# Layer 1's attention: the values product by batch in tiles of 64 rows, in two halves around the value projection

## What is computed

```python
qh = (q_in @ wq + bq).reshape(b, q_len, H, K)
kh = (kv_in @ wk + bk).reshape(b, t, H, K)
vh = (kv_in @ wv + bv).reshape(b, t, H, K)
kh = jnp.concatenate([kh, jnp.broadcast_to(bias_k, (b, 1, H, K))], axis=1)
vh = jnp.concatenate([vh, jnp.broadcast_to(bias_v, (b, 1, H, K))], axis=1)
scale = jnp.sqrt(jnp.asarray(K, q_in.dtype))
logits = jnp.einsum('bqhk,bthk->bhqt', qh, kh) / scale
weights = jax.nn.softmax(logits, axis=-1)
ctx = jnp.einsum('bhqt,bthk->bqhk', weights, vh).reshape(b, q_len, H * K)
return ctx @ wo + bo
```

## Time and profile before

| | |
|---|---|
| median of 3 runs | 1749.71 us (1749.53 to 1749.79) |
| the profiled execution's own time | 1759.38 us |
| its span in the trace | 1757.7 us |
| TensorE busy | 1592.3 us, 91% |
| VectorE busy | 920.9 us, 52% |
| ScalarE busy | 739.9 us, 42% |
| GpSimd busy | 429.2 us, 24% |
| mean granted clock of TensorE | 0.959 of full |

### The profile page before, as it was taken

One profiled execution on the slowest core, in us unless ns is written; L12 is line 12 of the kernel. 1 busy time (PEld: TensorE's weight loads), 2 busy tenths in 40 slices (PEclk: granted clock), 3 DMA queues, 4 the chain that ended last, 5 costly groups with the idle time before them and its releaser, 6 DMA issues. The chain is left out here.

```text
span 1757.7 us, 33325 instructions
## 1 busy us (share of the span) xinstructions
PE 1592.3 (91%) x13484; PEld 1355.6 (77%) x13484; DVE 920.9 (52%) x1912; ACT 739.9 (42%) x1393; POOL 429.2 (24%) x518
## 2 busy tenths in 40 slices
PE   5978999999999969999999999839978877999797
PEld 3656888888888858888888888729857756888597
DVE  6874444343434454252525353574469975776443
ACT  4653434343434334444343434332246643544321
POOL 2012020010110030110200200160058867663400
PEclk9998999999999989999999999959979988999899
DMA  3021010010000030000000100010050000000001
GB/s 101 1 64 45 1 49 1 7 43 1 25 13 1 1 101 9 25 25 1 25 25 1 37 1 1 31 39 1 0 133 1 2 1 2 3 3 2 1 1 48
DMA packets 48464, 38.24 MB, mean 22 GB/s; under 512 B 10626, under 2 KB 45384, under 8 KB 48200
## 3 DMA queue, kind: packets, MB, share of 16 engines
q1 hardware_dynamic: 48328, 36.30, 7.0%
HBM read 34.20 MB, written 2.10 MB: 21 GB/s over the span
## 5 line engine op out<-in xcount | busy, mean ns | idle before, releaser
L939 DVE TENSOR_REDUCE att_rmax<-psum 128x6 f32<-128x390 f32 (+1 forms) x96 | 49.2, 512 | 401.2 <-PE psum L771 401.2
L914 ACT ACTIVATE att_q_sb<-psum,split_cols 128x512 f32<-128x512 f32 x128 | 88.1, 688 | 295.8 <-PE psum L807 295.0
L852 PE MATMUL psum<-att_wo_hi,att_ot_hi 128*128 128x256 f32 x512 | 149.4, 292 | 2.8 <-DVE att_ot_lo L968 2.8
L852 PE MATMUL psum<-att_wo_lo,att_ot_hi 128*128 128x256 f32 x512 | 144.8, 283 | 0.0
L852 PE MATMUL psum<-att_wo_hi,att_ot_lo 128*128 128x256 f32 x512 | 144.8, 283 | 0.0
L835 PE MATMUL psum<-att_pt,att_v_sb 128*128 128x128 f32 x1024 | 122.2, 278 | 1.0 <-ACT att_pt L923 1.0
L835 PEld LDWEIGHTS psum<-att_pt,att_v_sb 128*128 128x128 f32 x1024 | 116.8, 192 | 3.3 <-issue 1.5
L917 ACT ACTIVATE att_k_sb<-psum,split_cols 128x512 f32<-128x512 f32 x128 | 88.2, 689 | 71.3 <-PE psum L807 71.3
L807 PE MATMUL psum<-split_feat_hi,att_wqk_hi 128*128 128x512 f32 x256 | 105.5, 412 | 12.8 <-DVE att_pt L933 12.8
L721 POOL CAST att_wqk_hi<-w_stage_qk 128x512 fp32r<-128x512 f32 x28 | 17.2, 613 | 401.4 <-PE psum L807 397.0
L977 DVE TENSOR_TENSOR g_x_res<-psum,g_x_res 128x256 f32<-128x256 f32 x128 | 54.3, 424 | 110.6 <-PE psum L852 77.7
(11 more groups left out here) (295 smaller groups left out, 4130.6 us busy)
## 6 DMA issues: line engine op xcount, KB each, us to landing
ln_wo<-in_L_xattn_wo SPq DMA_DIRECT2D x2, 2048.0 KB
w_stage_qk<-in_L_xattn_wq SPq DMA_DIRECT2D x32, 128.0 KB, 2.3
w_stage_qk<-in_L_xattn_wk SPq DMA_DIRECT2D x32, 128.0 KB, 2.8
w_stage_vo<-in_L_xattn_wv SPq DMA_DIRECT2D x8, 512.0 KB, 3.9
w_stage_vo<-in_L_xattn_wo SPq DMA_DIRECT2D x8, 512.0 KB, 3.9
...
```

The costliest lines, as they stand in the source:

```text
L852: mm = pe.matmul(o_ps[p % 2], a, b, start=(h == 0 and t == 0), stop=(not last and h == HG - 1 and t == 2))
L914: act.activation(q_sb[:, h, :], q_ps[:, :], ACT.Identity, bias=G.cols[:, i - 1, head:head + 1]).then_inc(q_ready, 1)
L939: dve.tensor_reduce(rmax[:, a:b], s_ps[group][:, :, :], X_AXIS, ALU.max).then_inc(max_done, 1)
```

## The change

- `pt` loses its zero halves: it is now 64 keys of either batch above one another and 64 columns for each chunk and head. The clearing of `pt` and its semaphore go. ScalarE copies each transposed pair with one instruction of 128 rows in place of two of 64.
- `context` takes a half (`pp`): two chunks. For each chunk, head and batch (`u`) it multiplies 64 rows of `v_sb` (128 stationary columns) with 64 columns of `pt`: 16 matmuls a half, 32 a block. Batch 0 of a chunk uses rows 0 to 63 and writes the first bank of `c_ps`, batch 1 rows 64 to 127 and the second bank.
- `c_ps` is now two banks, which are also those of the transposes (`t_ps`) and, for odd chunks, of the outputs. So half 1 has to wait until half 0 is copied out (`ot_ready`, now counted in halves).
- `context(j - 2, 0)`, `values(j - 1, 0)`, `context(j - 2, 1)`, `values(j - 1, 1)` follow one another, where there was `context(j - 2)` and `values(j - 1)`.
- `context_high` and `context_low` copy a half at a time (1024 elements a row), and `ot_hi` and `ot_lo` are laid out by chunk. The first output chunk waits for half 0, the others for half 1.
- The softmax steps on ScalarE and VectorE are put in another order around these copies.

```diff
-        pt = m.sb("pt", [P, HG, 2, 2, 2, T])
-        ot_hi, ot_lo = (m.sb(n, [P, HG, BLK], F32R) for n in ("ot_hi", "ot_lo"))
+        pt = m.sb("pt", [P, HG, 2, 2, T])
+        ot_hi, ot_lo = (m.sb(n, [P, PPB, HG, P], F32R) for n in ("ot_hi", "ot_lo"))
...
-        t_ps = [m.ps(f"t_ps{n}", (P, 2, 2, P)) for n in range(2)]
+        c_ps = m.ps("c_ps", (P, 2, PPB // 2, HG, T))
+        t_ps = c_ps.rearrange("p u c h t -> p u (c h t)").rearrange("p n (h a t) -> p n h a t", h=2, a=2)
...
-        c_ps = [q_ps, k_ps, flat[0], flat[1]]
-        o_ps = [o_full[:, 0:D], flat[1][:, 0:D]]
+        o_ps = [o_full[:, 0:D], c_ps[:, 1, 0, :, :].rearrange("p h t -> p (h t)")]
...
+        def by_half(ot, pp):
+            return ot[:, 2 * pp:2 * pp + 2, :, :].rearrange("p c h (u t) -> p u (c h) t", u=2)
...
-                def context(j):
-                    for copied in v_ready:
-                        pe.wait_ge(copied, 2 * j + 2)
-                    pe.wait_ge(q_ready, HG * min(j + 2, NI))
-                    pe.wait_ge(k_ready, HG * min(j + 2, NI))
-                    for h in range(HG):
-                        pe.wait_ge(pt_ready, 4 * j + 2 * (h // 2) + 2 if h < 2 else 4 * j + 4)
-                        for p in range(PPB):
-                            mm = pe.matmul(c_ps[h][:, p * P:(p + 1) * P], v_sb[:, p, h * K1:(h + 1) * K1],
-                                           pt[:, h, p // 2, p % 2, :, :].rearrange("p u t -> p (u t)"), start=True, stop=True)
-                        mm.then_inc(c_psum, 1)
+                def context(j, pp):
+                    pe.wait_ge(pt_ready, 2 * j + 2)
+                    if pp:
+                        pe.wait_ge(ot_ready, 2 * j + 1)
+                    else:
+                        for copied in v_ready:
+                            pe.wait_ge(copied, 2 * j + 2)
+                        if j:
+                            pe.wait_ge(x_added, PPB * j)
+                    for p in (2 * pp, 2 * pp + 1):
+                        for h in range(HG):
+                            for u in range(2):
+                                rows = slice(T * u, T * u + T)
+                                mm = pe.matmul(c_ps[:, u, p % 2, h, :], v_sb[rows, p, h * K1:(h + 1) * K1],
+                                               pt[rows, h, pp, p % 2, :], start=True, stop=True)
+                    mm.then_inc(c_psum, 1)
...
-                pe.wait_ge(pt_zero, 1)
...
-                        context(j - 2)
+                        context(j - 2, 0)
                     if 1 <= j <= NI:
-                        values(j - 1)
+                        values(j - 1, 0)
+                    if j >= 2:
+                        context(j - 2, 1)
+                    if 1 <= j <= NI:
+                        values(j - 1, 1)
...
-                            for u in range(2):
-                                half = slice(T * u, T * u + T)
-                                act.activation(pt[half, 2 * pair:2 * pair + 2, :, :, u, :].rearrange("p h a r t -> p (h a r) t"),
-                                               t_ps[pair][half, :, :, :].rearrange("p h a (r t) -> p (h a r) t", r=2),
-                                               ACT.Copy).then_inc(pt_ready, 1)
+                            act.activation(pt[:, 2 * pair:2 * pair + 2, :, :, :].rearrange("p h a r t -> p (h a r t)"),
+                                           t_ps[:, pair, :, :, :].rearrange("p h a t -> p (h a t)"), ACT.Copy).then_inc(pt_ready, 1)
...
-                dve.memset(pt[:, :, :, :, :, :].rearrange("p h a r u t -> p (h a r u t)"), 0.0).then_inc(pt_zero, 1)
...
+                def context_low(j, pp):
+                    dve.wait_ge(ot_high, 2 * j + pp + 1)
+                    dve.tensor_tensor(by_half(ot_lo, pp), c_ps[:, :, :, :, :].rearrange("p u c h t -> p u (c h) t"),
+                                      by_half(ot_hi, pp).bitcast(F32), ALU.subtract).then_inc(ot_ready, 1)
```

83 lines of the change are left out of this document (40 added, 43 removed).

## The result

| kernel | median of its runs, us | lowest to highest | beside the kernel before |
|---|---|---|---|
| before, runs beside the changed kernel | 1749.62 | 1748.61 to 1749.79 (4) | |
| changed | 1768.53 | 1767.43 to 1770.94 (4) | ratio 1.0112, interval 1.0099 to 1.0124 |

A forecast was written before the change was run, and what follows sets the result against it. TensorE's own time was taken to bound each pass. Terms 14.1 + 1.1 + 3.4 - 5.5 + 0 = +13.1 us, carried over to the runs' median of 1749.71, gave 1762.8 us; range 1752 to 1780, the sum's own 1757 to 1768.

The forecast's parts named there:

- The product gains nothing: Values product in each pass: a pair of half-depth records takes 0.112 us, as one full record does; 0 us.
- pairs at 0.060: Rival on the values product: half-depth loads take half the time or overlap further, 53 us less, 1710 us; chance 8%.
- loads in turn: Rival on the values product: loads of two row halves take turns, 0.224 a pair, 115 us more, 1878 us; 3%.
- Changes of tile shape: Borders between full and row tiles around the product: 0.47 us a pass, 30 passes, 14.1 us more.
- the turned bias: Last group, 3 passes an attention: bias transposes between scores and product add a full-to-row change, 6 x 0.19 = 1.1 us.
- The new wait: Second half's product in a pass waits until the first half is copied out; 0.5 us spare, so 0 us.
- The rival in which VectorE's copy comes too late: Before a pass's second half: VectorE's strided copy takes 2.32, 18 us more in all, 1781 us; chance 11%.
- The start: Start of each attention: TensorE no longer waits for the memset of pt, 2.75 us saved, twice: -5.5 us.
- The end: End of each attention: no projection hides the last block's wait for copies; +1.7 us, twice: 3.4.

The follow-up runs named there:

- the later wait: Kernel before, only ScalarE's first copy into the probabilities' buffer waits for the memset: 1739.87 us (ratio 0.9959), in a second lot 1743.70 us (0.9965).
- one-piece row tiles: Kernel before, its product kept in one piece but each batch over its own 64 rows, no zero blocks or memset: 1780.15 us, ratio 1.0184.
- first experiment: Changed kernel, half 2 of each attention's last product written into the queries' and keys' banks, so it needn't wait for half 1's copies: 1761.41 us, ratio 1.0075.
- full halves: Changed kernel's order, halves and copies, but each product over all 128 rows with the zero blocks and memset back: 1753.68 us, ratio 1.0026.

## Why the prediction was right in direction and 5.8 us short

The measured 1768.53 us lies within the range of 1752 to 1780 and 0.5 above the narrower 1757 to 1768 that was given to the sum by itself. The misses are nearly all in one term, the end of an attention.

- **The product gains nothing.** Right, with its mechanism: 0.112 us for a pair of row tiles as for a full matmul, the load being the limit. Halving the loaded columns gave 0.060, halving the stream left 0.110, and taking the rows one half after the other undid the overlap. Both rivals on the load (pairs at 0.060, loads in turn) fall.
- **Changes of tile shape.** Right: 0.50 us a pass in place of 0.47, and 0.70 in place of 0.66 with the turned bias; 15.8 over the kernel with the passes at both borders, where 14.1 + 1.1 were forecast. The kernel with full tiles in the same order has none of it. The Trainium skill, "TensorEngine Tiling (Array Packing)", "Key Properties", says that a change of tiling mode drains TensorE; the trace agrees in that each change costs time, and puts it at about 0.17 us each. From the start of a half's last record to the projection it is 0.20 where the prediction took a distance of 0.15.
- **The new wait.** Right: no idle time in a pass, and 0.57 us to spare where 0.5 was forecast. The rival in which VectorE's copy comes too late didn't come in either (its copy takes 1.23 us, near the 1.19 of the earlier trace rows and far from the 2.32).
- **The start.** -3.2 for each attention in place of -2.75: the next in line was GpSimd's att_wqk_lo, as forecast, but it released TensorE 0.4 us earlier than I had read from the pair of instructions in the earlier trace rows. But this was no gain of the row tiles; the kernel before has it for two moved waits.
- **The end. This is the term that was sized wrong**: "+1.7" for each attention measured 5.3 and 4.3 in the first profiled execution, 4.2 and 4.3 in the second. The 1.7 priced the wait and the longer copies at the full clock, and the end in the experiment with full tiles at clock 1.0 bears that out (1.8). What was left out is the granted clock: I took the earlier trace rows, an end at 1.0 throughout, as the state of a stretch that the change altered. In the profiled execution that is 3.6 + 2.6 = 6.2 us over the forecast; with -0.9 for the starts and +0.6 for the borders it leads from 13.1 to 19.0.

What brings the clock down at an end is, in the main, the idle time. The cleanest comparison has full tiles throughout and differs in the idle time ahead of the outputs alone: behind 2.01 us the clock fell at both ends, behind 1.41 at none of six (the kernel before, the later wait twice). Over all the profiles but that of one row half after the other, where the clock falls in the passes too:

| idle time of TensorE | clock fell |
|---|---|
| 2.0 to 2.5 us, at an end | 14 of 16 |
| 1.8 to 1.9 us, in a pass (one-piece row tiles; half the loaded columns) | 6 of 12 |
| up to 1.63 us, at an end, full tiles | 0 of 8 |
| up to 0.80 us, at an end, row tiles (first experiment) | 1 of 2 |

**Open** is what else decides. With full halves one end kept its clock and one lost it behind the same 2.46 us; with half the loaded columns one end kept it behind 2.48 and the other lost it only in the outputs; and in the first experiment one of two equal ends lost it behind 0.80. The length of the idle time alone doesn't settle it, so no exact limit can be read from these runs. The changed kernel's own four ends, and the two with half the moving columns, lost it every time.
